# A routed feed-forward block on one core: group tiles with fixed owners, hidden values turned on VectorE

## The reference

```python
def ffn(x):                                   # x: (2 * 256 rows of 256) per half; E=8 experts, top 2, I=640
    scores = sigmoid(xt @ w_router.T)         # (T, 8)
    topk_w, topk_i = top_k(scores, 2)
    topk_w = topk_w / topk_w.sum(-1)
    comb = zeros((T, 8)).at[arange(T)[:, None], topk_i].add(topk_w)
    gate = silu(einsum('th,eih->tei', xt, wg))
    up = einsum('th,eih->tei', xt, wu)
    out = einsum('te,teh->th', comb, einsum('tei,ehi->teh', gate * up, wd))
    return out + sum_j (silu(xt @ sg[j].T) * (xt @ su[j].T)) @ sd[j].T     # two shared experts

x = x + 0.5 * ffn(layernorm(x))               # x: (4, 256, 256) f32
x = x + ssm(layernorm(x))                     # softplus, a scan over 256 steps with 16 states, D * x
x = x + 0.5 * ffn(layernorm(x))               # the same weights again
```

## Time and profile before

| | us |
|---|---|
| median of 3 runs (506.65 to 507.55) | 506.81 |
| the profiled execution | 507.11 |
| its span in the trace | 505.3 |
| PE busy in it | 497.6 |

### The profile page before, as it was taken

How to read it: one execution, slowest core, us unless ns; L and a number is a source line. 1 busy time by engine, 2 the same in 40 slices (tenths; PEclk the granted TensorE clock), 3 DMA queues, 4 the chain that set the end, 5 groups by cost and what they waited for, 6 DMA issues and landing times.

```text
span 505.3 us, 11509 instructions
## 1 busy us (share of the span) xinstructions
PE 497.6 (98%) x4590; PEld 414.6 (82%) x4591; DVE 324.0 (64%) x621; ACT 148.7 (29%) x308; POOL 229.1 (45%) x206
## 2 busy tenths in 40 slices
PE   7999989999999999999999999999999999999997
PEld 6999986568979999557899799976589999955696
DVE  4746327213748998998679599999977533522225
ACT  1111122221155445453112643545421111112210
POOL 1050000413217998997354289999930650000041
PEclk9999999999999999999999999999999999999999
DMA  7958999511415565540121344746200242210022
GB/s 249 365 190 309 374 383 378 163 61 43 136 25 154 119 136 138 143 123 21 53 64 64 106 124 117 160 127 153 60 21 3 79 109 54 82 35 22 12 57 80
DMA packets 46050, 64.37 MB, mean 127 GB/s; under 512 B 13196, under 2 KB 29196, under 8 KB 45996
## 3 DMA queue, kind: packets, MB, share of 16 engines
q1 hardware_dynamic: 32988, 35.03, 25.9%
q10 hardware_dynamic: 9776, 20.06, 10.8%
q0 software_dynamic: 3232, 8.53, 5.4%
HBM read 46.95 MB, written 16.65 MB: 126 GB/s over the span
## 4 chain that ended last, share of the span: by engine, by line
PE 95%; ACTq 2%; DVE 1%; DMA 0%; ACT 0%; issue 0%; POOL 0%; POOLq 0%
PE ps L573 46%; PE ps L600 22%; PE ps L588 14%; PE ps L613 7%; PE ps L624 2%; ACTq L850 2%; PE ps L805 1%; PE ps L619 1%; PE ps L753 1%; DMA xres<-in_x 0%; PE ps L658 0%; PE ps L816 0%; ACT hb L855 0%; PE ps L798 0%; PE ps L668 0%
## 5 line engine op out<-in xcount | busy, mean ns | idle before, releaser
L573 PEld LDWEIGHTS ps<-xnp,w_gu 128*128 128x128 f32 x1280 | 149.4, 194 | 6.7 <-issue 4.8
L573 PE MATMUL ps<-xnp,w_gu 128*128 128x128 f32 x1280 | 152.2, 278 | 0.6 <-ACT xnp L970 0.6
L1120 DVE SCALAR_TENSOR_TENSOR hb<-hb,ps 128x640 f32<-128x640 f32 x68 | 55.4, 815 | 115.8 <-ACT hb L855 115.7
L600 PE MATMUL ps<-w_dn,hb 128*128 128x256 f32 x520 | 121.9, 380 | 0.0
L600 PEld LDWEIGHTS ps<-w_dn,hb 128*128 128x128 f32 x520 | 94.8, 191 | 11.4 <-issue 0.8
L855 ACT ACTIVATE hb<-ps 128x640 f32<-128x640 f32 x68 | 47.6, 700 | 176.9 <-PE ps L573 162.6
L573 PEld LDWEIGHTS ps<-xt,w_gu 128*128 128x128 f32 x800 | 92.5, 192 | 1.1 <-issue 0.2
L573 PE MATMUL ps<-xt,w_gu 128*128 128x128 f32 x800 | 92.8, 275 | 0.0
L1098 POOL TENSOR_TENSOR xna<-xna,hh 128x512 f32<-128x512 f32 x64 | 82.0, 1284 | 2.3 <-DVE hh L1176 2.3
L1171 DVE TENSOR_TENSOR_SCAN ps<-ps,region 128x512 f32<-128x512 f32 x64 | 78.3, 1223 | 2.9 <-ACT ps L949 2.6
L1064 POOL DMA_INDIRECT region<-yg_rows,pos x32 | 30.7, 959 | 104.2 <-DMA yg_rows<-ob 84.1
(11 more groups left out here) (109 smaller groups left out, 262.3 us busy)
## 6 DMA issues: line engine op xcount, KB each, us to landing
bcb<-bc_rows SPq DMA_DIRECT2D x22, 512.0 KB, 5.2
w_gu<-in_wg ACTq DMA_DIRECT2D x8, 640.0 KB, 11.2
w_gu<-in_wu ACTq DMA_DIRECT2D x8, 640.0 KB, 13.1
w_dn<-in_wd ACTq DMA_DIRECT2D x8, 640.0 KB, 13.8
region<-bc_rows SPq DMA_DIRECT2D x10, 512.0 KB, 5.2
yg_rows<-ob SPq DMA_DIRECT2D x20, 128.0 KB, 3.5
xg_rows<-bcb SPq DMA_DIRECT2D x1, 2176.0 KB, 11.7
xg_rows<-bcb ACTq DMA_DIRECT2D x1, 2176.0 KB, 19.9
```

The lines of the kernel that those rows point to most:

```text
L573: last = nc.tensor.matmul(gup(p)[:, c * P:(c + 1) * P], w_gu4[:, e, k, c * P:(c + 1) * P], x, start=(k == 0), stop=(k == KC - 1))
L600: ins = nc.tensor.matmul(outp(p), hb[:, p, c * P:(c + 1) * P], w_dn4[:, e, c, :], start=(c == 0), stop=(c == IC - 1))
L1120: nc.vector.scalar_tensor_tensor(out=h, in0=h, scalar=1.0, in1=gup(p)[:, 0:I], op0=ALU.add, op1=ALU.mult).then_inc(s_a, 1)
```

## The change

Three of the four mixed tiles of a segment become "tails" tiles: all four groups have fixed owners, so experts 0, 1 and 2 have 224, 224 and 192 rows of their own (before 192, 192, 160), the rest as before. One mixed tile with one free group stays, the last routed one. Tails tiles come in one load and go out in one store.

In segments 0 and 3 a tails tile is "blocked": the 32 rows of a group are stationary in all four column groups, and each column group takes a quarter of the features (every fourth run of 32). Gate and up are then cut into ten pieces a tile, of 160, 160, 160, 32, 128, 160, 160, 64, 96 and 160 columns, each for two halves of the contraction and four column groups. VectorE writes the product to PSUM and turns it in 32x32 blocks into `hb`, in the form that `down_mixed` wants; `turn_hidden` and ScalarE's copy drop out. In segments 1 and 2 tails tiles go on as mixed tiles did, with static weights for all groups.

The loads of weights are issued in another order and later: the nine issues of tiles 5 and 6 are spread over tiles 6 to 9, expert 2's down goes to tile 4, expert 4 to tile 5, and the fills of `xg_dram` and `yg_dram` go from tiles 7 and 10 to tiles 10 and 12.

```diff
-MIXED = [(5, 5, 5), (0, 0, 2), (1, 1, 3), (6, 6, 7)]
+TAILS = [(0, 0, 0, 3), (1, 1, 1, 7), (2, 2, 6, 6)]
+MIXED = [(5, 5, 5)]
...
-ROUTED = [("whole", e, e) for e in range(WHOLE)] + [("mixed", None, m) for m in range(MT)]
+ROUTED = ([("whole", e, e) for e in range(WHOLE)] + [("tails", None, m) for m in range(len(TAILS))]
+          + [("mixed", None, m) for m in range(MT)])
...
+def blocked(n):
+    return kind_of(n) == "tails" and segment(n) in (0, SEGS - 1)
+
+def turned_back(n):
+    return grouped(n) and not blocked(n)
...
-        LATE = {1: ((0, GATES),), 3: ((2, ALL),), 4: ((3, ALL), (4, ALL)), 5: ((5, GATES),),
-                6: ((5, DOWN), (6, DOWN), (7, DOWN))}
-        LATE_MID = {3: ((0, DOWN), (1, ALL)), 6: ((6, GATES), (7, GATES))}
+        LATE = {1: ((0, GATES),), 3: ((2, GATES),), 4: ((2, DOWN), (3, ALL)), 5: ((4, ALL),), 6: ((7, GATES),),
+                7: ((7, DOWN), (6, GATES)), 8: ((6, DOWN), (5, GATES)), 9: ((5, DOWN),)}
+        LATE_MID = {3: ((0, DOWN), (1, ALL))}
...
+            def gate_up_blocked(n, c0):
+                p, share = n % 2, I // 4
+                pieces = {0: ((0, 0, 0, 5),), 2: ((0, 1, 0, 5),),
+                          4: ((0, 2, 0, 5), (0, 3, 0, 1), (0, 3, 1, 5), (1, 0, 0, 5), (1, 1, 0, 5), (1, 2, 0, 2)),
+                          8: ((1, 2, 2, 5), (1, 3, 0, 5))}
+                for half, g, a, b in pieces[c0]:
+                    at = half * I + g * share
+                    for k in range(KC):
+                        w = w_gu4[:, owners_of(n)[g], k, half * I:(half + 1) * I].rearrange("p (c j u) -> p c j u", j=4, u=GROUP)
+                        for j in range(4):
+                            last = nc.tensor.matmul(gup(p)[j * GROUP:(j + 1) * GROUP, at + a * GROUP:at + b * GROUP],
+                                                    xt[:, p, k, g * GROUP:(g + 1) * GROUP], w[:, a:b, j, :],
+                                                    start=(k == 0), stop=(k == KC - 1))
+                return last
...
             down_mixed(n, free):
+                        at = j * (I // 4) + c * GROUP if blocked(n) else c * P + r
+                        ins = nc.tensor.matmul(outp(p)[r:r + GROUP, :], hb[:, p, at:at + GROUP], w,
...
             PE, first(n):
-                if kind_of(n) == "mixed":
+                if turned_back(n):
                     pe.wait_ge(s_h, n + 1)
                     turn_hidden(hb[:, q, :], hidden_turned(q)).then_inc(s_tr6, 1)
...
             PE, second(n):
+                if grouped(n):
+                    pe.wait_ge(s_ht, grouped_upto(n))
+                    if blocked(n):
+                        rows_of(n)
+                    down_mixed(n, free.get(n)).then_inc(s_dn, 1)
...
             ACT, first(n):
-                if kind_of(n) == "mixed":
-                    act.wait_ge(s_tr6, mixed_upto(n))
+                if turned_back(n):
+                    act.wait_ge(s_tr6, turned_back_upto(n))
...
             ACT, send_late(n):
-                if n == 7:
+                if n == 10:
                     act.wait_ge(s_zero, 1)
                     clear(xg_dram[1], CLEARED, s_clr[1])
-                if n == 10:
+                if n == 12:
                     clear(yg_dram[0][OVER_ROW:, :], OVER_CLEARED, s_clr[2])
...
             DVE, hidden(n):
-                nc.vector.tensor_tensor(h, h, gup(p)[:, I:GU], ALU.mult).then_inc(s_h, 1)
+                if blocked(n):
+                    nc.vector.tensor_tensor(gup(p)[:, 0:I], h, gup(p)[:, I:GU], ALU.mult).then_inc(s_h, 1)
+                    dve.wait_ge(s_h, n + 1)
+                    nc.vector.transpose(h, gup(p)[:, 0:I]).then_inc(s_ht, 1)
+                else:
+                    nc.vector.tensor_tensor(h, h, gup(p)[:, I:GU], ALU.mult).then_inc(s_h, 1)
```

More of the change, by code:

```diff
@@ L23 @@
 GROUP = 32
-MIXED = [(5, 5, 5), (0, 0, 2), (1, 1, 3), (6, 6, 7)]
+TAILS = [(0, 0, 0, 3), (1, 1, 1, 7), (2, 2, 6, 6)]
+MIXED = [(5, 5, 5)]
 MT = len(MIXED)
[L27 to L30, removed]
+ROW_ORDER = [("whole", 0), ("tails", 0), ("whole", 3), ("whole", 1), ("tails", 1), ("whole", 2), ("tails", 2),
+             ("whole", 4), ("mixed", 0)]
+ROW_OWNERS = [e for kind, k in ROW_ORDER
+              for e in ((k,) * 4 if kind == "whole" else TAILS[k] if kind == "tails" else MIXED[k])]
+FIRST_ROW = {tile: P * k for k, tile in enumerate(ROW_ORDER)}
 FREE0 = GROUP * len(ROW_OWNERS)
-OWN = [g for tile in MIXED for g in tile]
+OWN = [g for tile in TAILS + MIXED for g in tile]
 ROOM = [(P if e < WHOLE else 0) + GROUP * OWN.count(e) for e in range(E)]
@@ L85, in last_routed @@
 def last_routed(s):
-    return s * SEG_TILES + max(j for j, t in enumerate(ORDERS[s]) if t[0] == "mixed")
+    return s * SEG_TILES + max(j for j, t in enumerate(ORDERS[s]) if t[0] != "shared")
 def by_vector(n):
@@ L101, in turned, with grouped, owners_of, turned_back_upto @@
     return sum(1 for m in range(n + 1) if routed(m))
-def mixed_upto(n):
-    return sum(1 for m in range(n + 1) if kind_of(m) == "mixed")
+def grouped(n):
+    return kind_of(n) in ("tails", "mixed")
+def blocked(n):
+    return kind_of(n) == "tails" and segment(n) in (0, SEGS - 1)
+def turned_back(n):
+    return grouped(n) and not blocked(n)
+def owners_of(n):
+    return TAILS[index_of(n)] if kind_of(n) == "tails" else (None,) + MIXED[index_of(n)]
+def turned_back_upto(n):
+    return sum(1 for m in range(n + 1) if turned_back(m))
+def grouped_upto(n):
+    return sum(1 for m in range(n + 1) if grouped(m))
 def loads(n, q):
@@ L590, in gate_up_mixed @@
                 return last
+            def gate_up_blocked(n, c0):
[12 more added lines that the diff above has]
+                return last
             def gate_up(n, free, c0, c1):
[L593 removed]
+                if blocked(n):
+                    return gate_up_blocked(n, c0)
+                return gate_up_mixed(n, free, c0 * P, c1 * P) if grouped(n) else gate_up_fixed(n, c0, c1)
             def down_fixed(n, ranks=None):
@@ L634, in first_use @@
                 if kind_of(n) == "mixed":
-                    if index_of(n) == 0:
-                        for e in range(E):
-                            weights_in(e, k)
+                    for e in range(E):
+                        weights_in(e, k)
+                elif kind_of(n) == "tails":
+                    for e in sorted(set(owners_of(n))):
+                        weights_in(e, k)
                 elif kind_of(n) == "whole" or index_of(n) == 0:
```

21 lines of the change are left out of this document (10 added, 11 removed).

## The result

The changed kernel takes 501.53 us (median of 4 runs, 500.67 to 501.93), the kernel before, measured beside it, 506.88 (4 runs, 506.65 to 507.55): 0.989 of it, 95% interval 0.9873 to 0.9907. The profiled execution took 501.24 us, its span is 499.5 us where before's was 505.3. The forecast was 501.2 with a span of 499.7.

A forecast was written before the change was run, and what follows sets the result against it. TensorE, busy for 497.6 of 505.3 us, was taken to bound the kernel. Terms 5.0 + 1.8 - 0.9 - 0.3 = 5.6 us, from median 506.81 to 501.2 (span 499.7); range 499.8 to 504.8, own range 499.8 to 502.8.

The forecast's parts named there:

- Turns that drop out: Six blocked tiles in segments 0 and 3 lose TensorE's `turn_hidden`, saving 0.84 us each, 5.0 us in all.
- Ten pieces: Gate and up of the six blocked tiles, cut into shorter rounds, costs 0.15 us a tile, 0.9 us, bounds 0 and 4.4.
- The rival with 110 ns a round: Every gate-and-up round in blocked tiles costs at least 110 ns: 4.4 us lost, gain 2.4, time 504.4; chance 0.15.
- The feed: Rival: blocked tiles' records reach TensorE no faster than 36 ns each, 8.4 us lost, 508.4 us; chance 0.09.
- Weights later: Later weight issues let ScalarE's copies arrive in time, ending two TensorE waits in segment 0: 1.8 us gained, 1.5 to 1.9.
- "G": GpSimd's "G" in segment 0, behind the later fill and "S", comes late: 0.3 us lost, bounds 0 and 0.8.
- The rival's price: Fill landing 3 us later than thought makes adds, layernorm and TensorE's turns 2.2 us late: 503.2 us; chance 0.08.
- VectorE's turn: Blocked tiles' turn on VectorE, at most 1.1 us, is covered by 4 us of TensorE work and costs nothing.
- Fixed owners and register loads: One free group suffices, the overflow loop stays shut, and `free_expert` register loads on TensorE leave no gap: nothing.

The follow-up runs named there:

- the variant with the early register: Changed kernel with the free group's expert read two tiles earlier and tile 13 waiting only for expert 5's weights: 500.91 us, in a second comparison 500.28.
- the one execution that shows it: Changed kernel with the fill of the second row buffer issued one tile later, after tile 11: one execution of 506.5 us, span 504.7.

## Why the prediction was right, and where it was off

The time was right: 5.35 us gained in the median and 5.8 in the span, with 5.6 forecast. But some of its terms were wrong, and that their errors cancelled is luck.

- *Turns that drop out*, 5.0 us: right. Segment 3 gained 2.3 us from three turns of 0.84, less 0.2 for the pieces. Undoing the spread returns some 5 us.
- *Ten pieces*: 0.07 us a tile, 0.4 in all, for 0.9, in the bounds. The shape of the trace's records explains it: a round is paid by its columns, with some 20 ns above at the most (46 for 27 at 32 columns). The rival with 110 ns a round falls with it. So does the estimate that the prediction made of the Trainium skill ("TensorEngine Tiling (Array Packing)", Instruction Overhead), some 60 cycles of overhead a matmul, paid by the four records of a round one after another, some 100 ns: the trace has 46 ns a round where four column groups work side by side.
- *The feed*: rated at 0.09, from 34 ns a record on. It did not strike in after, but its mechanism is real: 27 ns a matmul with its weight load at best, when instructions run out, and a stop of 1.09 us in the variant with the old issue order. The prediction took 36 ns from the `score` step, which shows no feed at all, and had no row for the real limit. The 62 ns that the Trainium skill ("TensorE: Matmul & The Clock Gate", Wait — 56ns, not 53.3ns?) gives a matmul with hardware decode off are not what this trace has, as the prediction said. But the limit at 27 ns stands 20% from the break-even of 34, not far off.
- *Weights later*: 1.8 us forecast, 2.0 seen in the stretch, with the copies in time and the two waits gone, as the step said. The old order put back lost 0.36 us there and 1.09 in a stop elsewhere, so the number is right as an account of the two traces and not as a price of the order.
- *"G"*: 0.3 us forecast, nothing lost. The later fill landed by 101.69, where 104.8 was the estimate, and "S" was over before the last store. What failed was the size of the fill's step: its duration (12.1 us at most; the trace has 9.7 from issue to landing) and its start (92.9; it was issued at 91.70). The rival's price was too low: 3.5 us of lateness cost over 5 in the one execution that shows it.
- *VectorE's turn*: nothing, right; 0.85 us where at most 1.1 were allowed, and the cover shown.
- *Fixed owners and register loads*: "nothing" was the term that failed. The prediction read that `free_expert` had no gap on the chain of before, in tiles whose pieces filled 7.44 us. The change puts a tails tile ahead of the first mixed one where a fixed tile stood (blocked or not: the variant without blocked tiles has the gap too). There the sequencer is 1.46 us ahead of TensorE when it comes to the sixteen waits and the load, where it was 2.13 ahead in before, and the load lies beside the later fill (1.08 to 1.10 us there, 0.49 to 0.50 in the variants with no fill under way). It cost 1.25 us in segment 0, and nothing in segment 3, where the weights need no waits and the load takes 0.3 us.

What held the sum together: 1.25 us lost there stand against 0.5 in the pieces, 0.3 in "G", 0.2 in the issues and 0.65 in the first 68 us, which no step explains, less 0.15 in the rest. The 0.65 are no more than the spread of single executions: the same point came at 67.17 us in another execution of after and at 68.33 in the variant with the early register, for 67.56 and 68.21.

## What to carry to other kernels

When a tile's records get smaller and more, count instruction bytes against the time of the tile beside columns: here 64 bytes an instruction, 16 KB in 3.46 us at best. Tiles at 83% of it ran free in the changed kernel and stopped for 1 to 2 us in two of its variants; at 122% the kernel lost three times what the change had won. Steps that a sequencer does between tiles (waits, a register loaded from DRAM) were free only as far as it was ahead; where they show, put them some tiles early. A transfer that others queue behind is priced by what stands behind it, and a wait of 2 us cost more than its length here, as the granted clock was lower after it.

## What the runs showed of the hardware

- TensorE's instructions arrive in packets of 16 KB. When the stream ran out, 256 instructions followed each other every 3.46 us at best; the six stops given above ended 2.3 to 2.4 us after a packet set out. Under DMA load at 0.89 one packet was 7 us behind another (98.81 and 105.83).
- A load of a register from DRAM on TensorE's sequencer took 1.08 us beside the 2176 KB fill (0.62 beside that of before), 0.5 without it and 0.3 in later segments. Records of waits that had long been fulfilled, one or two semaphores in each, came 0.106 us apart; with seven of them gone the gap was 0.74 us shorter.
- TensorE waited 2.13 and 2.25 us for VectorE in two variants. The granted clock was 0.58 in the window behind the one (132 to 136 us) and 0.78 in the window around the other (364 to 370 us), a mean of the levels of 2.4 and 1.2 GHz, and the next records took 1.4 to 2.3 times as long (a down product 3.46 us for 2.32; five turns 1.29 for 0.55, the gate and up behind them 3.79 for 2.68). After the gap of 1.05 us in the kernel after it stayed at 2.4 GHz.
- A 32x32 turn of 640 columns from PSUM takes VectorE 0.85 us, about the time of the product of the same size (0.83).
